# Decay exponents from GpSimd instead of a matmul, and re-tiled small products, in a gated delta rule kernel

## The reference

```python
q, k, v = causal_dwconv(x @ Wq.T), causal_dwconv(x @ Wk.T), causal_dwconv(x @ Wv.T)   # 4 taps
g, beta = log_sigmoid(x @ Wg.T), sigmoid(x @ Wb.T)
k = k / norm(k); q = q * 64 ** -0.5
for t in range(T):                       # state S: 64 x 64 for each batch and head
    delta = outer(v_t, k_t) - outer(S k_t, k_t)
    S = exp(g_t) * S + beta_t * delta
    o_t = S q_t
x = layernorm(x + o @ Wo.T)
```

## Time and profile before

| | before |
|---|---|
| median of 3 runs | 1878.1 us (1876.3 to 1878.67) |
| span of the profiled execution, first to last instruction | 1786.9 us |
| the same execution's time outside its span | not in the profile; 1878.1 - 1786.9 = 91.2 us for the median run |
| PE busy | 1610.3 us, 90% |
| DVE busy | 1209.9 us, 68% |
| ACT busy | 891.0 us, 50% |
| POOL busy | 852.7 us, 48% |

### The profile page before, as it was taken

One profiled execution on the slowest core, in us unless ns is written; L12 is line 12 of the kernel. 1 busy time (PEld: TensorE's weight loads), 2 busy tenths in 40 slices (PEclk: granted clock), 3 DMA queues, 4 the chain that ended last, 5 costly groups with the idle time before them and its releaser, 6 DMA issues. The chain is left out here.

```text
span 1786.9 us, 73925 instructions
## 1 busy us (share of the span) xinstructions
PE 1610.3 (90%) x31244; PEld 1234.8 (69%) x31244; DVE 1209.9 (68%) x3061; ACT 891.0 (50%) x2282; POOL 852.7 (48%) x1070
## 2 busy tenths in 40 slices
PE   7478999999999999999999999975899999889990
PEld 6135766667767667667667676664799998788870
DVE  1388888888888888888888888831666666222225
ACT  1276666667666667667766676611111111232333
POOL 0033443434434344343434434410577777677775
PEclk9799999999999999999999999978999999999995
DMA  7236455556555555565564555444665541599758
GB/s 279 83 72 124 106 118 125 126 112 117 134 117 111 122 120 118 117 135 113 115 136 103 116 127 114 93 88 140 200 192 162 182 148 41 156 257 248 149 87 294
DMA packets 520889, 245.44 MB, mean 137 GB/s; under 512 B 423376, under 2 KB 485456, under 8 KB 519664
## 3 DMA queue, kind: packets, MB, share of 16 engines
q1 hardware_dynamic: 368464, 200.72, 42.9%
q10 hardware_dynamic: 133632, 20.98, 6.3%
q0 software_dynamic: 18464, 19.03, 6.0%
HBM read 169.29 MB, written 71.37 MB: 135 GB/s over the span
## 5 line engine op out<-in xcount | busy, mean ns | idle before, releaser
L375 PE MATMUL delta_p_j<-delta_xt,delta_w 128*128 128x512 f32 x768 | 385.9, 625 | 30.5 <-DMA delta_xt<-in_xt 18.0
L575 DVE SCALAR_TENSOR_TENSOR delta_kq<-delta_hist,cw,delta_kq 128x512 f32<-128x512 f32 x384 | 295.5, 770 | 31.2 <-ACT delta_kq L723 24.2
L716 ACT ACTIVATE delta_hist<-delta_p_j 128x512 f32<-128x512 f32 x192 | 114.8, 598 | 253.2 <-PE delta_p_j L375 249.9
L889 POOL TENSOR_TENSOR delta_sd<-state,eg_end 128x256 f32<-128x256 f32 x128 | 104.4, 815 | 282.7 <-DVE state L655 282.7
L375 PEld LDWEIGHTS delta_p_j<-delta_xt,delta_w 128*128 128x128 f32 x768 | 131.5, 191 | 145.4 <-issue 111.7
L1396 POOL DMA_INDIRECT slot_tokens<-mix_tokens,mix_slot x192 | 189.9, 989 | 62.5 <-issue 52.6
L436 PEld LDWEIGHTS delta_p_i<-delta_kkq,rt 64*64 64x64 f32 x4096 | 130.4, 135 | 74.1 <-DVE delta_kkq L639 68.2
L864 POOL TENSOR_SCALAR delta_n<-delta_n 128x8 f32<-128x8 f32 x64 | 15.5, 242 | 299.1 <-DVE delta_n L606 299.1
L436 PE MATMUL delta_p_i<-delta_kkq,rt 64*64 64x32 f32 (+1 forms) x4096 | 143.3, 214 | 15.2 <-DVE delta_kkq L639 14.2
L1166 PE MATMUL mix_p_h<-mix_wo,w 128*88 128x128 f32 x1024 | 126.5, 277 | 14.7 <-ACT mix_wo L1352 13.6
L1166 PEld LDWEIGHTS mix_p_h<-mix_wo,w 128*88 128x88 f32 x1024 | 116.4, 158 | 31.1 <-ACT mix_wo L1352 28.6
(11 more groups left out here) (148 smaller groups left out, 3627.2 us busy)
## 6 DMA issues: line engine op xcount, KB each, us to landing
delta_xd<-x_scratch SPq DMA_DIRECT2D x256, 128.0 KB, 4.0
delta_w<-in_wqkv SPq DMA_DIRECT2D x64, 416.0 KB
w<-in_w SPq DMA_DIRECT2D x64, 352.0 KB
delta_eg<-eg_rows SPq DMA_DIRECT2D x128, 130.0 KB, 3.1
n_scratch<-delta_kkq ACTq DMA_DIRECT2D x128, 128.0 KB
mix_ot<-ot SPq DMA_DIRECT2D x16, 1024.0 KB, 5.8
w<-in_w SPq DMA_DIRECT2D x64, 176.0 KB
ot<-delta_o SPq DMA_DIRECT2D x32, 256.0 KB, 3.8
```

Source lines behind the costliest of these rows:

```text
L375: mm = pe.matmul(p_j[:, :], w[e][:, (ch * 3 + n) * 128:(ch * 3 + n) * 128 + 128], xt[m // 8 % 2][:, ch * 512:ch * 512 + 512], start=ch == ...
L575: ve.scalar_tensor_tensor(out, view(hist[e], i * 2 * 518 + tap, (259, 2), (1, 256)), cw[:, column:column + 1], out, ALU.mult, ALU.add).the ...
L716: ac.activation(view(hist[e], n * 518 + 3, (259, 2), (1, 256)), p_j[:, :], ACT.Copy)
L889: po.tensor_tensor(view(sd, 0, (128, 2), (C, 2), (1, C)), view(state, first_pair(group) * 128, (C, 2), (128, 2), (1, C)), view(s.eg_end, g ...
```

## The change

The matmul `exponents` and its operands go. SP loads for each macro the row c_j of its units, spread over all 64 partitions of each half (2 DMAs, each 64 partitions x 2 KB), into a new tile `span`; POOL subtracts c_i (kept from the gates phase in `cum`) and adds a constant mask (`C_LATER`), in `exponent`, two instructions in place behind `roots`; ACT's `decay` reads `span`. `project` of v waits for the last tap of k, no more for `decay`. The last two inverse products load only the 32 or 16 columns of weights whose results are wanted. The output products take the two batches to the two halves of the result's partitions, one bank for each head of the pair, in the order `OUTPUTS`, and `store_o` has four DMAs for three.

```diff
+        OUTPUTS = [(0, 0), (1, 1), (0, 1), (1, 0)]
@@ load_rows
                 for sh in range(2):
-                    sp.dma_start(view(arg_l[e], sh * C, (1, C), parts=(64 + sh * 8, 8)),
-                                 bass.AP(s.g_rows, m * 1024 + sh * 512, [[C, 8], [1, C]])).then_inc(r_in[e], 16)
-                sp.dma_start(view(arg_r[e], 0, (1, 512), parts=(80, 2)),
-                             bass.AP(s.g_rows, m * 1024, [[512, 2], [1, 512]])).then_inc(r_in[e], 16)
+                    sp.dma_start(span[e][64 * sh:64 * sh + 64, :],
+                                 bass.AP(s.g_rows, m * 1024 + sh * 512, [[0, C], [1, 512]])).then_inc(r_in[e], 16)
@@ project
-                if n == 1 and m == 0:
-                    pe.wait_ge(tap_k, 1)
-                if n == 1 and m >= 1:
-                    pe.wait_ge(exped, m)
+                if n == 1:
+                    pe.wait_ge(tap_k, m + 1)
@@ exponents
-                pe.matmul(p_j[:, :], view(arg_l[e], 0, (1, 128), parts=(0, 82)), view(arg_r[e], 0, (1, 512), parts=(0, 82)),
-                          start=True, stop=True).then_inc(arg, 1)
@@ inverse_ry1, inverse_ry2
-                by_unit(rt, kkq, ring(m), 32, 32, ry1_done)
+                by_unit(rt, kkq, ring(m), 32, 32, ry1_done, 32)
-                by_unit(rt, kkq, ring(m), 48, 16, ry2_done)
+                by_unit(rt, kkq, ring(m), 48, 16, ry2_done, 16)
@@ chain_update
-                    for b in range(NB):
-                        for sh in range(2):
-                            mm = pe.matmul(view(p_d, b * 512 + q * 256 + c * C, (1, C), parts=half(sh)),
-                                           view(u, (b * 2 + q) * C, (1, C), parts=half(sh)),
-                                           view(kkq, ring(group * 2 + q) + 512 + b * 256 + c * C, (1, C), parts=half(sh)),
-                                           start=False, stop=c == 3, skip_group_check=True)
+                    for b, h in OUTPUTS:
+                        mm = pe.matmul(view(p_d, h * 512 + q * 256 + c * C, (1, C), parts=half(b)),
+                                       view(u, (b * 2 + q) * C, (1, C), parts=half(h ^ b)),
+                                       view(kkq, ring(group * 2 + q) + 512 + b * 256 + c * C, (1, C), parts=half(h ^ b)),
+                                       start=False, stop=c == 3, skip_group_check=True)
@@ decay
-                ac.wait_ge(arg, m + 1)
+                ac.wait_ge(arg, 2 * m + 2)
-                ac.activation(view(ex[e], 1, (C + 1, 8), (1, C)), view(p_j, 0, (C, 8), (1, C)), ACT.Exp).then_inc(exped, 1)
+                ac.activation(view(ex[e], 1, (C + 1, 8), (1, C)), view(span[e], 0, (C, 8), (1, C)), ACT.Exp).then_inc(exped, 1)
@@ gpsimd
+            def exponent(m):
+                e = m % 2
+                po.wait_ge(r_in[e], 32 * (m // 2 + 1))
+                po.tensor_tensor(view(span[e], 0, (C, 8), (1, C)), view(span[e], 0, (C, 8), (1, C)),
+                                 view(s.cum, m * 8, (1, 8), (0, C)), ALU.subtract).then_inc(arg, 1)
+                po.wait_ge(arg, 2 * m + 1)
+                po.tensor_tensor(view(span[e], 0, (C, 8), (1, C)), view(span[e], 0, (C, 8), (1, C)),
+                                 view(const, C_LATER, (0, 8), (1, C)), ALU.add).then_inc(arg, 1)
...
                     roots(before)
+                if is_macro(m):
+                    exponent(m)
```

More of the change, by code:

```diff
@@ L209, in delta_phase @@
         yv = two("yv", 512)
-        eg, ex, arg_l, arg_r = two("eg", 520), s.ex, s.arg_l, s.arg_r
+        eg, ex, span = two("eg", 520), s.ex, two("span", 512)
         kpv, kkq, kqg = sb("kpv", 8 * 1024), sb("kkq", 8 * 1024), sb("kqg", 8 * 1024)
@@ L326, in store_o @@
                 sp.wait_ge(o_done, group + 1)
-                sp.dma_start(bass.AP(s.ot, at, [[NTOK, 128], [128 * NTOK, 2], [1, SPAN]]),
-                             view(src, 0, (SPAN, 2), (1, SPAN))).then_inc(o_out[group % 2], 16)
-                for sh in range(2):
-                    sp.dma_start(bass.AP(s.ot, at + (sh ^ 1) * 64 * NTOK + T, [[NTOK, 64], [128 * NTOK, 2], [1, SPAN]]),
-                                 view(src, 512, (SPAN, 2), (1, SPAN), parts=half(sh))).then_inc(o_out[group % 2], 16)
+                for b in range(NB):
+                    for h in range(2):
+                        sp.dma_start(bass.AP(s.ot, at + h * 64 * NTOK + b * T, [[NTOK, 64], [128 * NTOK, 2], [1, SPAN]]),
+                                     view(src, h * 512, (SPAN, 2), (1, SPAN), parts=half(b))).then_inc(o_out[group % 2], 16)
             load_weights(0)
@@ L430, in products, with by_unit @@
                 mm.then_inc(prods, 1)
-            def by_unit(lhs, rhs, at, first, count, done):
+            def by_unit(lhs, rhs, at, first, count, done, rows=C):
                 for g in range(8):
                     for sh in range(2):
-                        mm = pe.matmul(view(p_i, g * C + first, (1, count), parts=half(sh)),
-                                       view(lhs, g * C, (1, C), parts=half(sh)),
+                        mm = pe.matmul(view(p_i, g * C + first, (1, count), parts=(64 * sh, rows)),
+                                       view(lhs, g * C, (1, rows), parts=half(sh)),
                                        view(rhs, at + g * C + first, (1, count), parts=half(sh)), start=True, stop=True)
@@ L478, in chain_state @@
                 for q in range(2):
-                    for b, h in QUADS:
-                        mm = pe.matmul(view(p_d, b * 512 + q * 256 + c * C, (1, C), parts=half(h ^ b)),
+                    for b, h in OUTPUTS:
+                        mm = pe.matmul(view(p_d, h * 512 + q * 256 + c * C, (1, C), parts=half(b)),
                                   view(state, ((pair + q) * 2 + b) * C, (1, C), parts=half(h)),
@@ L1472, in program @@
             s.beta, s.kd, s.eg_end, s.noff, s.rt = (asb(n, 512) for n in ("beta", "kd", "eg_end", "noff", "rt"))
-            s.arg_l, s.arg_r = [asb(f"arg_l{i}", 128) for i in range(2)], [asb(f"arg_r{i}", 512) for i in range(2)]
+            s.cum = asb("cum", 512)
             s.cw, s.state, s.carry = asb("cw", NPAIR * 3 * (TAPS + 1)), asb("state", 1024), asb("carry", NPAIR * 18)
```

44 lines of the change are left out of this document (8 added, 36 removed).

## The result

The changed kernel takes 1904.06 us (median of 4 runs, 1901.55 to 1913.63). The kernel before, on the same chip, takes 1877.2 us. The ratio is 1.0164, with a 95% interval from 1.0131 to 1.0197: **1.6% slower, 27 us**. The forecast was 1882, slower by 4 us, with a range from 1840 to 1912. Sign and range hold; 23 of the 27 us are missing from its sum, and most of this text looks for them.

What follows compares the result with a forecast made beforehand. PE was taken as the bound, DVE close behind. PE loses 2.6 us a slot, but DVE's slot grows to 17.34: +8 us over 56 slots, -4 at the start, so 1882 against 1878.1; range 1840 to 1912.

Steps and rivals of the forecast that it cites:

- PE was the bound and DVE close behind: Delta phase before the change: PE sets the 17.25 us slot, DVE's stream fills 15.73 us of it.
- Whatever is taken off PE is worth 1.5 us a slot at most: Delta phase: gain capped at 17.25 - 15.73 = 1.5 us a slot, with DVE's order and work unchanged.
- PE's parts: PE's slot: exponent matmul 1.06, outputs 0.56, inverse products about 1.0 us off; sum 2.6, at least 1.06.
- POOL's parts and the port: POOL gains 2.3 us a macro; DVE's taps of q, held by POOL's SBUF reads, lose 1.56 us a slot.
- The slot of 17.34, and 17.40 with stalls: Delta slot after: DVE's 15.73 + 1.56 + 0.05 = 17.34; with remaining PE stalls, +0.15 a slot over 17.25.
- Together +4: Whole kernel: +8 us over 56 slots, -4 us over three starting slots without the matmul and Exp in the chain.
- TensorE's clock: Rival, chance 0.13: a less busy PE falls to 1.2 GHz at times; 1900 us, or +60 and more.
- one each 100 us costing 2 us, +20: The clock rival's price: one 6.7 us low-clock stretch per 100 us, 2 us each, giving 1900 us.
- By its own signs: Wrong if taps keep 0.75 us, the clock falls in the steady part, or a new DVE wait appears.
- DMAs at nothing: Spread loads, 2 x 128 KB a macro instead of 8 KB: hidden by the whole slot, under 1 us otherwise.

Runs made afterwards that it cites:

- products_alone: Kernel before with only the re-tiled output products, narrower inverse products and four store DMAs, decays still by the matmul: 1761.41 us, 0.9844 of before.
- pool_writes: products_alone plus two useless POOL fills a macro at the place of `exponent`, which read nothing: 1771.37 us, 0.9908 of before.
- pool_reads: products_alone plus two useless POOL instructions a macro at the place of `exponent`, of the real forms, reading SBUF: 1804.10 us, 1.0086 of before.
- dead_matmul: Changed kernel plus one useless matmul a slot (128 rows, 512 columns) where the exponent matmul used to be: 1803.83 us, 1.0090 of before.
- after_again: The changed kernel, unchanged, run again on the chip where before takes 1789.37 us: 1816.71 us, 1.0154 of before.
- before_again: The kernel before, unchanged, run for a second profile: 1783.76 us (one run).
- exponents_alone: Changed kernel with the re-tiled outputs, narrower inverse products and four store DMAs undone, decays from POOL: 1820.60 us, 1.0177 of before.
- ahead_of_roots: Changed kernel with POOL's `exponent` one place earlier, between `weight` and `roots`: 1817.23 us, 1.0152 of before.
- aligned: ahead_of_roots with a wait, so that `exponent` starts as DVE ends the two taps of v: 1881.75 us, 1.0070 of before.

## Why the prediction was right, and where its sum fell short

**The balance, as a chain of kernels.** Each step changes one thing, by ratios to before, times 1788 us:

| step | from | to | us |
|---|---|---|---|
| products re-tiled | 1 | 0.9844 (products_alone) | -28 |
| two instructions more on POOL, which only write | 0.9844 | 0.9908 (pool_writes) | +11 |
| they read SBUF | 0.9908 | 1.0086 (pool_reads) | +32 |
| spread loads; the matmul no more needed but still as long | 1.0086 | 1.0090 (dead_matmul) | +1 |
| that matmul gone | 1.0090 | 1.0154 (after_again) | +11 |

The last row is 12.9 us by the medians; the two ratios stand on two sets of runs of before. The sum is +27 us.

**PE was the bound and DVE close behind.** Right. "Whatever is taken off PE is worth 1.5 us a slot at most" was true and far too generous: 0.38 us came from 0.9 taken off (products_alone). The step treated DVE's 15.73 us as a stream that would close up, and left out PE's waits for DVE inside the inverse. Here this cost nothing, as DVE's price at the port came first.

**PE's parts.** The outputs gave 0.35 us (0.57 to 0.38, 0.56 to 0.40) for a forecast of 0.56. The 0.29 of `chain_state`, from which the forecast was made, is a group with more small products behind it; ahead of a matmul over the whole array the same eight products hold PE for 0.38 to 0.40. The inverse products gave 0.22 and 0.35, 0.57 for a forecast of 1.0. The step was that the weight loads set the pace and that a group would shrink with the columns to 0.43 and 0.25; measured 0.62 and 0.50. In after a load of 32 columns takes 110 ns and one of 16 takes 90, where one of 64 takes 135 to 140: about the 26 and 39 ns less that were reckoned from the earlier trace rows. But 110 and 97 of 136 ns are not a half and a quarter; a group shrinking with these would take 0.69 and 0.61, and the measured ones lie nearer to that. The Trainium skill (TensorE: Matmul & The Clock Gate, section LDWEIGHTS), by whose rule the 1.0 was to hold, has a load's time in proportion to its columns. The traces agree that fewer columns load faster, not that the time is in proportion. It made no difference to the sum.

**POOL's parts and the port.** Right or close in each number: 1.04 and 1.26 us; `decay_state(one)` 1.07, `off_diagonal` 1.46; `off_diagonal` before PE needs it, with no wait for it among PE's. The price was 1.56 us a slot forecast; the taps grew by 1.42 (after, 4.61 to 6.03) to 1.71 (dead_matmul, to 6.32) on the mean of the slots, and by 1.81 in the one shown above. pool_writes against pool_reads shows that the cause is the reading of SBUF.

**The slot of 17.34, and 17.40 with stalls.** dead_matmul is the changed kernel with PE's clock at full, which is what the sum assumed, though with 1 us more of work on PE: 17.46 us. The model of DVE was good to 0.06 us.

**"Together +4".** dead_matmul has +16 instead. Of these 12 us, 6 are a slot longer by 0.26 than before_again's 17.20 instead of by 0.15. The other 6 are the start: I had put -4 us there, for the matmul that leaves the chain of the three first slots. The mask of macro 6 starts at 177.7 us in before_again, at 180.1 in dead_matmul and at 179.4 in after_again, 2 us later and not 4 earlier (179.3 in the first profile of before, so the 6 is known to some 2 us). The masks ahead of it say where it went. That of macro 2 starts at 116.1 us in before_again and at 113.7 in dead_matmul, so 2.4 of the 4 us did arrive; they were lost in the four slots up to macro 6, to which the sum gave no price. Two stretches at 1.2 GHz fall there in dead_matmul, five ahead of macro 6 in after_again, none in before_again.

**The clock, which had 0.13.** This is the step that failed. The price of "TensorE's clock" was left outside the sum as a rival, with "one each 100 us costing 2 us, +20". It came in every run that has no long matmul at that place (after, exponents_alone, ahead_of_roots, aligned: 12 to 20 stretches), and hardly in those that have one (0 to 3). In after_again it is 20 stretches in 996 us, one each 50 us, for 13 us together. The evidence had been in the earlier trace rows, where a slot with PE 77% busy had a clock of 0.78 and others as busy had 1.00. I read this as undecided. With the average falling from 98% to a forecast 83%, it should have been part of the likeliest case. The rival's 1900 was nearer to the 1904 than the forecast's 1882, but by luck: it had half as many stretches at three times the price.

**By its own signs.** The prediction called itself wrong if the clock fell in the steady part or if DVE got a new wait. Both came: 16 to 20 stretches, and the waits of `horner` and the mask for PE. The mechanism at the port was right; that the time lies in the range owes something to its width of 72 us, which was there for the rivals.

**DMAs at nothing.** Right for this kernel, for the reason given (the whole slot hides them) only as long as DVE sets the pace; 0.23 us a slot where it doesn't.

**Left open.** In the phase after the delta rule the slower chip shows a lower clock (0.80 from 1240 to 1420 us of after), and nearly all of the 5% between the chips lies in that phase: the last mask is at 1192.0 us of after and at 1192.4 of after_again, whose spans are 1899.8 and 1815.0. Why chips differ was not studied. The best version among these kernels is products_alone, 0.9844 of before: it beats both kernels.

## What to carry to other kernels

Before work is moved to an engine that is half idle, look at who shares its port at that place of the slot: 2.3 us on a half idle POOL took 1.4 to 1.7 us from DVE because three taps with two SBUF operands stood beside it, and little where DVE read PSUM (0.35 us, in aligned). Time taken off the bounding engine is worth only what its partner's waits allow, so price each part alone: here one half of the change was worth 1.6% and the other cost more than that. And an engine whose clock falls behind its waits is not made idle for free: ask what long waits it will have after the change, and try it with a dead product of the old length.

## What the runs showed of the hardware that was not expected

- A useless matmul of 512 columns in each slot made a kernel 0.7% faster (1816.7 to 1803.8 us), with PE's busy share at 92% instead of 87%, and 0 instead of 20 stretches at 1.2 GHz.
- On POOL, an instruction over 128 x 512 elements takes 1.04 us where its second operand is one value repeated along 64 columns, and 1.26 where it is a row of 64 different columns.
- Halving the columns of a group's 64-column weights took its time from 0.85 to 0.62 us, quartering them to 0.50 (loads of 135, 110 and 90 ns).
- The same output products, ahead of the same matmul over the whole array, hold PE for 0.38 us a group over all four quarters of the array and for 0.57 over two. Ahead of other small products the next group starts after 0.23 us.
